# A decoder megakernel on one NeuronCore: the second rotary product of the latent queries, or four transfers that exchange its rows

## What is computed

```
half = 32
x1, x2 = (x[..., :half], x[..., half:])            # x = (q @ W_dq) @ W_qr, one head
rot = concat([x1 * cos - x2 * sin, x1 * sin + x2 * cos])
score = (q_latent . k_latent + rot(q) . rot(k)) / sqrt(192)
```

## Time and profile before

| | |
|---|---|
| median of 3 runs | 701.72 us (700.37 to 703.38) |
| span of the profiled execution | 699.1 us |
| PE, DVE, ACT, POOL busy in it | 94%, 68%, 50%, 51% |
| scan stage, roughly | from 220 us to 311 us |
| latent attention, roughly | from 311 us to 499 us |
| last layer's experts, roughly | from 499 us to 690 us |

### The profile page before, as it was taken

The page is one execution under the profiler, slowest core; times in us unless marked ns, Lnnn a source line. Parts: engine busy times, 40 slices in busy tenths (PEclk is TensorE's granted clock), DMA queues, the critical chain, the costliest instruction groups (busy, mean ns, idle before and its releaser), DMA issues.

```text
span 699.1 us, 12877 instructions
## 1 busy us (share of the span) xinstructions
PE 653.7 (94%) x4654; PEld 515.7 (74%) x4654; DVE 477.9 (68%) x1097; ACT 353.0 (50%) x815; POOL 355.7 (51%) x482
## 2 busy tenths in 40 slices
PE   9989989889999888789999999999999999999994
PEld 6856668858576545457888888887579888888884
DVE  6578878494284999998866767775375556666555
ACT  4655536150635746356877877776452222222224
POOL 5325416671102795555786766766424444444421
PEclk9999999999999999899999999999999999999998
DMA  8000007001003000000000200000102111111001
GB/s 283 2 2 3 1 2 300 1 1 50 1 0 86 16 1 0 2 1 1 1 2 1 69 1 2 2 1 2 68 24 68 46 45 46 46 46 46 0 1 61
DMA packets 10352, 23.32 MB, mean 33 GB/s; under 512 B 2033, under 2 KB 5074, under 8 KB 9906
## 3 DMA queue, kind: packets, MB, share of 16 engines
q1 hardware_dynamic: 10002, 22.24, 9.7%
q10 hardware_dynamic: 288, 0.26, 0.1%
HBM read 21.45 MB, written 1.05 MB: 32 GB/s over the span
## 4 chain that ended last, share of the span: by engine, by line
PE 72%; DVE 19%; ACT 4%; issue 2%; POOL 1%; DMA 1%; POOLq 0%; SPq 0%; DVEq 0%; ACTq 0%
PE psum L463 43%; DVE A L1555 7%; PE psum L1126 5%; PE psum L1137 4%; PE psum L524 4%; DVE A_rounded L1480 2%; PE psum L577 2%; PE psum L946 2%; PE psum L619 1%; DVE A L1404 1%; DVE stats L1277 1%; DVE x_tok L1274 1%; PE psum L583 1%; PE psum L593 1%; PE psum L956 1%
## 5 line engine op out<-in xcount | busy, mean ns | idle before, releaser
L463 PE MATMUL psum<-parts 128*128 128x256 f32 (+2 forms) x1472 | 253.7, 327 | 2.4 <-DVE C L1591 1.1
L463 PEld LDWEIGHTS psum<-parts 128*128 128x128 f32 (+1 forms) x1472 | 219.9, 190 | 31.5 <-issue 3.9
L2198 POOL TENSOR_SCALAR probs<-probs,row_rec 128x256 f32<-128x256 f32 x128 | 70.1, 560 | 47.5 <-DVE row_rec L1348 44.5
L2112 ACT ACTIVATE A<-psum 128x512 f32<-128x512 f32 x44 | 26.3, 598 | 115.5 <-PE psum L463 115.5
L1784 ACT ACTIVATE probs<-probs,neg_max 128x256 f32<-128x256 f32 x128 | 63.8, 500 | 32.8 <-DVE neg_max L1339 32.8
L1555 DVE TENSOR_TENSOR_SCAN A<-decay,psum 128x256 f32<-128x256 f32 x128 | 75.4, 661 | 4.9 <-PE psum L946 4.9
L1674 DVE TENSOR_TENSOR A<-A,psum 128x512 f32<-128x512 f32 x44 | 30.1, 687 | 70.6 <-ACT A L2112 58.4
L1339 DVE CUSTOM_DVE_ANT_0 probs<-psum,ctxT 128x256 f32<-128x256 f32 x128 | 48.9, 419 | 38.9 <-PE psum L463 36.7
L463 PE MATMUL psum<-parts,A_rounded 128*128 128x256 f32 x404 | 65.3, 288 | 3.5 <-DVE A_rounded L1480 3.5
L463 PEld LDWEIGHTS psum<-parts,A_rounded 128*128 128x128 f32 x404 | 56.3, 196 | 4.9 <-DVE A_rounded L1480 2.8
L1712 DVE TENSOR_TENSOR parts<-A,parts 128x512 fp32r<-128x512 f32 x44 | 48.9, 1111 | 0.8 <-ACT parts L2119 0.7
(11 more groups left out here) (265 smaller groups left out, 1280.9 us busy)
## 6 DMA issues: line engine op xcount, KB each, us to landing
A<-in_experts SPq DMA_DIRECT2D x12, 384.0 KB, 3.1
C<-in_experts SPq DMA_DIRECT2D x10, 384.0 KB, 3.0
A<-in_w_o SPq DMA_DIRECT2D x1, 2048.0 KB, 13.1
x_tok<-in_x_tok SPq DMA_DIRECT2D x1, 1024.0 KB, 7.1
ctxT<-in_ctxT SPq DMA_DIRECT2D x1, 1024.0 KB, 10.7
A<-in_w_uqT SPq DMA_DIRECT2D x1, 768.0 KB, 7.1
out<-x_tok SPq DMA_DIRECT2D x6, 128.0 KB, 1.8
xT<-in_xT SPq DMA_DIRECT2D x2, 256.0 KB, 3.6
```

The costliest lines, as they stand in the source:

```text
L463: ins = mm(o, left[l], right[r], start=first and n == 0, stop=last and n == 2, skip_group_check=True)
L2198: last = pool.tensor_scalar(pr, pr, row_rec[:, u % RING[n], j:j + 1], 1.0, ALU.mult, ALU.mult)
```

## The change

The product with the exchanged weights is gone, with its weights, their load and their split on GpSimd. VectorE now multiplies the one plain product twice: first by the sines (into a buffer of its own, `sine_part`, two slots), then by the cosines. The sines' signs are turned round in the table. SyncE then issues four transfers a pair, each of 32 partitions by 256 words (32 KB), which carry the rows of `sine_part` to the exchanged rows of `ropes`. A pair's transfers wait until those of the pair before have landed. GpSimd's addition waits for all four.

The pairs are also made earlier: pair n in step max(n, 2n-6) on TensorE, VectorE and ScalarE, and added on GpSimd one step after that. So pairs 4, 5 and 6 are made in the steps 4, 5 and 6, and from 7 on each is made two steps earlier than before; the addition comes one step earlier than before (for pair 4 one step later, for pair 5 in the same step). `HIGH_AT` and `LOW_AT` stay. The first three expert chunks are issued behind the transfers of pair 20.

Some semaphores are merged (`qk` and `v` into `qkv`, `m_g` and `m_u` into `m_gu`, `warm` into `const_p`), with counts that stand for the same events; these lines are left out below.

```diff
@@ buffers and order
+        with nc.sbuf_tensor("parts_plain", [P, 10752], f32) as parts_plain:
+            pass
         parts = sb("parts", [P, 10752], f32r)
...
-        wqr_swp = view(C, 4608, [QC, NPAIR, P])
...
-        wqr_swp_parts = view(parts, 2048, [QC, 2, NPAIR, P])
+        sine_part = view(parts_plain, 2048, [P, 2, S])
...
-        QUERIES_AT = {2 * (n - FIRST) + 4: n for n in range(FIRST, B * NPAIR)}
+        QUERIES_AT = {max(n, 2 * n - 6): n for n in range(FIRST, B * NPAIR)}
+        ADDED_AT = {u + 1: n for u, n in QUERIES_AT.items()}
+        QUARTERS = ((0, 32), (32, 0), (64, 96), (96, 64))
+        RAW_BEHIND = 20
@@ SyncE
-            load("wqr_swp", wqr_swp)
...
-            sp.wait_ge(sem("fin"), 4 * NT + 1)
-            for c in range(FCH):
-                if c == RAW - 1:
-                    sp.wait_ge(sem("a4_av"), B * NPAIR)
+            def swap_halves(n):
+                sp.wait_ge(sem("q_sine"), n + 1)
+                if n:
+                    sp.wait_ge(sem("q_swap"), 64 * n)
+                for to, at in QUARTERS:
+                    sp.dma_start(ropes[to:to + 32, n % 2, S:2 * S], sine_part[at:at + 32, n % 2, :]
+                                 ).then_inc(sem("q_swap"), 16)
...
+            for n in range(B * NPAIR):
+                swap_halves(n)
+                if n == RAW_BEHIND:
+                    sp.wait_ge(sem("fin"), 4 * NT + 1)
+                    for c in range(RAW - 1):
+                        load_expert(c)
+            sp.wait_ge(sem("a4_av"), B * NPAIR)
+            for c in range(RAW - 1, FCH):
@@ TensorE, query_pair
-                product3(rope[:, 0:S], left(wqr_raw_parts), rhs, True, True)
-                product3(rope[:, S:2 * S], left(wqr_swp_parts), rhs, True, True).then_inc(sem("q_rope"), 1)
+                product3(rope[:, 0:S], left(wqr_raw_parts), rhs, True, True).then_inc(sem("q_rope"), 1)
@@ VectorE, rotate_pair
-                tt(ropes[:, n % 2, 0:S], rope[:, 0:S], tab_qc, ALU.mult)
-                tt(ropes[:, n % 2, S:2 * S], rope[:, S:2 * S], tab_qs, ALU.mult).then_inc(sem("q_mul"), 1)
+                tt(sine_part[:, n % 2, :], rope[:, 0:S], tab_qs, ALU.mult).then_inc(sem("q_sine"), 1)
+                tt(ropes[:, n % 2, 0:S], rope[:, 0:S], tab_qc, ALU.mult).then_inc(sem("q_mul"), 1)
@@ GpSimd, add_pair, scan units and add_next
                 pool.wait_ge(sem("q_mul"), n + 1)
+                pool.wait_ge(sem("q_swap"), 64 * (n + 1))
...
-                if 25 <= n < 28:
-                    last = split_of(wqr_swp_parts, wqr_swp, n - 25)
-                    if n == 27:
-                        last.then_inc(sem("q_split"), 1)
...
-                if u in QUERIES_AT:
-                    if u:
-                        pool.wait_ge(sem("a4_norm"), u)
-                    add_pair(QUERIES_AT[u])
+                if u in ADDED_AT:
+                    pool.wait_ge(sem("a4_norm"), u)
+                    add_pair(ADDED_AT[u])
@@ tables
-    o["tab_qs"] = o["tab_ks"] * scale
+    o["tab_qs"] = -o["tab_ks"] * scale
```

More of the change, by code:

```diff
@@ L560, in heads_of_tile @@
                                     [wqk_parts[:, r, dc, :] for r in range(2)], dc == 0, dc == DC - 1)
-                last.then_inc(sem("qk"), 1)
+                last.then_inc(sem("qkv"), 1)
                 if i == 0:
@@ L568, in heads_of_tile @@
                                     [wv_parts[:, r, dc, :] for r in range(2)], dc == 0, dc == DC - 1)
-                last.then_inc(sem("v"), 1)
+                last.then_inc(sem("qkv"), 1)
             def row_scores(o, qt):
@@ L642, in _ @@
             zeros = small[:, 0:3, :].rearrange("p a b -> p (a b)").bitcast(bf16)
-            pe.wait_ge(sem("warm"), 1)
+            pe.wait_ge(sem("const_p"), 1)
             for i in range(12):
@@ L649, in _ @@
                     loaded(pe, "ident")
-                    pe.wait_ge(sem("const_p"), 1)
+                    pe.wait_ge(sem("const_p"), 2)
                 if i >= 2:
@@ L813, in mixing @@
                 if k < 2:
-                    pe.wait_ge(sem("const_p"), 4)
+                    pe.wait_ge(sem("const_p"), 5)
                     pe.wait_ge(sem("f_alTs"), k + 1)
@@ L1033, in _ @@
                     if n == 5:
-                        pe.wait_ge(sem("const_p"), 3)
+                        pe.wait_ge(sem("const_p"), 4)
                     state_sums(n // 4 - 1)
@@ L1066, in _ @@
                 if n == 29:
-                    pe.wait_ge(sem("q_split"), 3)
+                    pe.wait_ge(sem("q_split"), 2)
                     pe.wait_ge(sem("operand_lo"), QC_AT + 1)
@@ L1168, in product_to @@
                                     [x_parts[:, r, dc, hh] for r in range(2)], dc == 0, dc == DC - 1)
-                last.then_inc(sem(("m_g", "m_u")[w]), 1)
+                last.then_inc(sem("m_gu"), 1)
             def gate_up(place):
@@ L1360, in rotate @@
             def rotate(i):
-                dve.wait_ge(sem("qk"), i + 1)
+                dve.wait_ge(sem("qkv"), 2 * i + 1)
                 if i >= 2:
@@ L1519, in _ @@
             dve.wait_ge(sem("f_lg"), 1)
-            dve.wait_ge(sem("const_p"), 2)
+            dve.wait_ge(sem("const_p"), 3)
             softmax_small(bank[4][:, 0:64].rearrange("p (i w) -> p i w", w=8), 8).then_inc(sem("f_alpha"), 1)
@@ L1670, in product_of_tile @@
                 dve.wait_ge(sem("m_silu"), place + 1)
-                dve.wait_ge(sem("m_u"), place + 1)
+                dve.wait_ge(sem("m_gu"), 2 * place + 2)
                 if k >= AHEAD:
@@ L1808, in _ @@
                 if i == 0:
-                    act.wait_ge(sem("const_p"), 1)
-                act.wait_ge(sem("v"), i + 1)
+                    act.wait_ge(sem("const_p"), 2)
+                act.wait_ge(sem("qkv"), 2 * i + 2)
                 af(v_sum[:, i, :, 0:HD0], bank[2 + i % 2][:, 0:D].rearrange("p (h w) -> p h w", w=HD0), ACT.Copy
@@ L2055, in _ @@
                     j = n - 28
-                    act.wait_ge(sem("q_split"), 3)
+                    act.wait_ge(sem("q_split"), 2)
                     af(key_parts[j][:, 0, :], (keys_a, keys_b)[j], ACT.Copy).then_inc(sem("k_high"), 1)
@@ L2107, in silu @@
             def silu(place):
-                act.wait_ge(sem("m_g"), place + 1)
+                act.wait_ge(sem("m_gu"), 2 * place + 1)
                 if place >= 2:
@@ L2201, in _ @@
             heads = qk_tok.rearrange("p i (h w) -> p i h w", w=PAD)
-            pool.memset(small[:, 0:3, :], 0.0).then_inc(sem("warm"), 1)
+            pool.memset(small[:, 0:3, :], 0.0).then_inc(sem("const_p"), 1)
             pool.memset(v_sum[:, :, :, HD0], 1.0)
@@ L2230, in _ @@
                         loaded(pool, "ctxT")
-                        pool.wait_ge(sem("v"), NT)
+                        pool.wait_ge(sem("qkv"), 2 * NT)
                     both_parts(ctx_parts[:, :, DC * (o - 1):DC * o, :], ctxT[:, o - 1]).then_inc(sem("r_ctx"), 1)
@@ L2369, in split_weights @@
                 if c >= 2:
-                    pool.wait_ge(sem("m_u"), 3 if c == 2 else 2 * c - 2)
+                    pool.wait_ge(sem("m_gu"), 6 if c == 2 else 4 * c - 4)
                 link(pool.tensor_copy(gu_parts[:, c % 2, 0, :], w[:, 0:GU]))
@@ L2458, in laid_out @@
     swp = (r + 32) % 64
[L2459 to L2461 removed]
+    o["wqr_raw"] = a["L1_xattn_W_qr"].reshape(96, 8, 128)
     o["w_dq"] = chunks(a["L1_xattn_W_dq"])
```

6 lines of the change are left out of this document (4 added, 2 removed).

## The result

The changed kernel takes 704.81 us (median of 18 runs, 701.9 to 706.85) against 701.17 us before (18 runs, 699.61 to 706.27): ratio 1.0041, interval 1.0027 to 1.0055. The forecast was 695.2 us, range 692.3 to 700. The time is outside the range and on the other side of no change.

The account below looks back on a forecast made before the run. TensorE was taken to set the attention's pace: -9.9 for matmuls, +0.3 ScalarE, +2.4 start, +0.7 steps 4 to 8, summing to -6.5 us, from the 701.72 us median to 695.2 us; range 692.3 to 700.

Parts of the forecast that it names:

- What bounds the kernel, and the matmuls: Attention: TensorE sets the pace; 28 pairs lose 0.355 us of query matmuls each, 9.9 us off.
- ScalarE as the next bound: Attention: pairs without output product fall to about ScalarE's own load, so 0.3 us of the gain is taken away.
- L: Transfer round, from the end of the sines' multiplication to the fourth landing: 3.2 us, bounds 2.6 and 4.0.
- The steady pairs: Middle of the attention: the transfer round and GpSimd's addition fit into existing slack, so they cost nothing.
- The start: Ahead of the attention: two successive transfer rounds delay pair 3's rotation and the first maximum, costing 2.4 us.
- 2L - 4.0: The start's cost, by the length L of a transfer round: 2.4 us at L = 3.2.
- rival B: Start: TensorE idles near 315 to 318 us, its clock falls, +3 us, 698.2 us; chance 0.15.
- Steps 4 to 8: Early attention: an extra rotation and low_pair(4)'s wait make VectorE 1.5 us late; half reaches TensorE, 0.7 us.
- C: Attention: ScalarE or VectorE sets the new pace, no pair under 5.3 us, 700.6 us; chance 0.09.
- D: Attention: the four transfers follow one another and SyncE's round sets the pace, about 765 or 716 us; chance 0.08.

Follow-up runs that it names:

- e8: Kernel before, with the exchanged-weights product left out for pairs 4 to 31 only, no transfers: 693.65 us, ratio 0.9895 to the kernel before.
- e7: Changed kernel with eight transfers of 16 rows a pair instead of four of 32: 749.34 us, ratio 1.0684 to the kernel before.
- e2: Changed kernel with pairs 0 to 3 by the exchanged-weights product again, transfers from pair 4 on: 700.82 us, ratio 0.9999 to the kernel before.
- e5: Changed kernel with unread matmuls filling TensorE's waits, 12 ahead of the attention, 16 in step 6: 702.66 us, ratio 1.0022 to the kernel before.
- e3: Changed kernel with latent_pair ahead of high_pair in ScalarE's order within a step: 700.58 us, ratio 0.9987 to the kernel before.
- e4: Changed kernel with pairs 0 to 5 by the exchanged-weights product, transfers for pairs 6 to 31: 694.5 us, ratio 0.9895 to the kernel before.
- e9: Changed kernel with pairs 0 to 7 by the exchanged-weights product, made in the earlier order, transfers from pair 8: 693.94 us, ratio 0.9894 to the kernel before.

## Why the prediction was wrong, point by point

The forecast's terms, put into the stretches of the profile (its four pairs ahead of step 11 give -1.4, the pair moved forward +0.7, the waits of steps 4 to 8 +0.7):

| stretch | forecast, us | profile, us |
|---|---|---|
| start | +2.4 | +5.5 |
| steps 4 to 10 | 0 | +6.4 |
| from step 11 on | -8.9 | -9.35 |
| sum | -6.5 | +2.6 |

The ratio of the runs gives +2.9 us.

**What bounds the kernel, and the matmuls.** Right in the steady part: 5.09 us a pair, forecast 5.1, and 9.35 us won from step 11 on (216 query matmuls became 138; 78 x 0.118 = 9.2 us). The 0.3 us for ScalarE as the next bound were not paid: pairs without an output product take 402.41 - 398.18 = 4.23 us in the chain. Over-counted for the pairs of steps 4 to 10, where e8 won 0.5 us instead of 1.4.

**L.** Landing was right (1.85 us, forecast 1.8). The issues were not: 0.59 + 0.04 us each instead of 0.47, so a usual round is 3.7 us and not 3.2, within the stated bounds; the first one had an issue of 2.0 us and took 5.2 us, outside them. The estimate of 3.5 us from the Trainium skill, "DMA: Bandwidth & Descriptors", section "Anatomy of one DMA", was nearer than mine for the usual round, and little nearer for the first; that section is written for transfers issued by GpSimd, and these are SyncE's. (By the prediction's own terms it would have made the sum 0.75 us worse, not 0.9.) The page's section "Rules for kernel authors" says that two transfers to separate partition halves serialize. For the whole time of a transfer the trace does not show that: four in a row would take 4 x 1.85 = 7.4 us, and took 3.7. Whether their bytes move in turn it does not tell.

**The steady pairs.** Right: nothing was paid there, and e7 shows what it takes to pay.

**The start.** The mechanism, landing after landing ahead of pair 3's rotation, was right as far as it went, the size was not: 2.4 us forecast, 5.5 in the profile, 3 to 4 in the runs of e2. With the usual round of 3.7 us the prediction's own term, 2L - 4.0, gives 3.4 us, which is what the chain of e5 shows. The one long issue added 1.4 us. The last 0.7 us are rival B's mechanism (first scores 3.75 us instead of 1.73). I had given it 0.15 and put the idle time behind the sums; it lay ahead of the first scores, because TensorE waits for pair 0's addition itself, which the sum had not followed. The rows could have told: I read the chain before step 4 as VectorE's and ScalarE's, but in rows 7 `sums_out(1)` waits 0.74 us for TensorE's sums, and the chain before goes through TensorE's first scores.

**Steps 4 to 8: the step that failed.** I followed what stands behind `low_pair(4)` on VectorE and took 0.7 us. On ScalarE the same wait, `high_pair(4)`, has `latent_pair(5)` behind it, and TensorE cannot begin pair 6 before that copy. The profile has 6.4 us more from the outputs to step 11. TensorE waits 3.83 us at pair 6, and e3, which changes this order alone, gives back 3.9 in the profile and 3.8 in the time. Of the rest some 2 us are the pair moved forward (e4 and e9 have them too), of which the sum had 0.7 as matmuls; for VectorE's wait, the one that was followed, 0.5 us are left, near the 0.7 forecast. Worked out for ScalarE, the wait could have been found: `high_pair(4)` ends at 331.4 in the prediction's own frame, the copy 0.7 us later, while TensorE was due at pair 6's queries about 328 (step 6's come at 327.29 us in the trace before, with pair 5's work moved ahead of them).

**Rivals.** Neither C nor D happened, and B in its mechanism, at another place. The time is inside the 705.2 us up to which I had called it no change (0.16); 18 runs of each tell it apart from none, on the side that I had given 0.08. It came there by two costs that I had both named and both sized too small; no rival held them together.

## What to carry to other kernels

A transfer put into a chain in place of work on an engine costs nothing where the schedule has steps to spare and its whole round where it has not: list the first uses, ahead of the pipeline and in its first steps, apart from the steady ones, and there keep the old way (e4, e9: 1.0 to 1.1% faster than before, where the change everywhere is 0.4% slower). For each wait that a change adds, go through every engine on which something waits for the same event, and ask what stands behind it in that queue and who needs that; the costly wait was two hops from the one that was looked at. And an idle TensorE can have a second price, in the matmuls that follow; here most of it lay beside other engines' work (0.7 us in the chain, for 2.0 us in the first scores alone).

## What the runs showed of the hardware

- Four transfers of 32 KB within SBUF on one queue: 0.55 to 0.64 us from issue to issue, the last landed 1.85 us after its issue. Halved to 16 KB the landing is still 1.81 us (e7): time goes by their number.
- Single issues and landings take much longer now and then: an issue of 2.0 us in the first burst of the changed kernel, a landing of 3.39 us in the second round of e3.
- TensorE's clock fell to the lower level behind waits of 2.0 to 3.8 us between short groups of matmuls, and filling one wait kept it up only until the next (e5). The Trainium skill, "TensorE: Matmul & The Clock Gate", section "HAM oscillation", describes this falling back for waits for transfers; the trace agrees, with 3.75 us instead of 1.73 for the same eight matmuls behind pair 0's round. It fell in the same way behind a wait of 2.57 us for VectorE (to 0.52 from 286 us on, rows 9).
- Executions of the same instructions differ in the clock: 0.67 or 1.00 from 220 to 230 us, 3.3 us of span, which makes one profile a poor measure of a difference of 3 us.
